# Second layer with its weights held in the array and 512 tokens moving, the result by features, and x and the result turned by 32x32 transposes and DRAM round trips

## The reference

```python
nx = _layer_norm(x, ln_gamma, ln_beta)
q = nx @ Wq;  k = prototype_bank @ Wk;  v = prototype_bank @ Wv
weights = softmax(einsum('bth,bph->btp', q, k) * H ** (-0.5))
evidence = einsum('btp,bph->bth', weights, v)
combined = concatenate([nx, evidence, anchor], axis=-1)          # 3H wide
router_probs = softmax(combined @ router_W + router_b)           # E = 3 experts
h = silu(einsum('btc,ecr->bter', combined, e_w1) + e_b1)         # R = 512 per expert
expert_out = einsum('bter,erh->bteh', h, e_w2) + e_b2
routed = sum(expert_out * router_probs[..., None], axis=-2)
g = sigmoid(silu(combined @ gate_w1 + gate_b1) @ gate_w2 + gate_b2)
return x + g * (routed @ out_w + out_b)
```

## Time and profile before

| | |
|---|---|
| median of 3 runs | 466.26 us (465.49 to 466.45) |
| span of the profiled execution | 462.2 us; the median run is 4.1 us above it |
| PE busy | 451.3 us, 98% |
| DVE busy | 263.2 us, 57% |
| ACT busy | 236.0 us, 51% |
| POOL busy | 143.4 us, 31% |
| SyncE's DMA queue | 31.76 MB in 24256 packets, 26.4% of the 16 engines' span |

### The profile page before, as it was taken

The page is one execution under the profiler, slowest core; times in us unless marked ns, Lnnn a source line. Parts: engine busy times, 40 slices in busy tenths (PEclk is TensorE's granted clock), DMA queues, the critical chain, the costliest instruction groups (busy, mean ns, idle before and its releaser), DMA issues.

```text
span 462.2 us, 7383 instructions
## 1 busy us (share of the span) xinstructions
PE 451.3 (98%) x2771; PEld 400.3 (87%) x2771; DVE 263.2 (57%) x574; ACT 236.0 (51%) x361; POOL 143.4 (31%) x200
## 2 busy tenths in 40 slices
PE   4999999999999999999999999999999999999995
PEld 4588888898988899898988999898988998988895
DVE  3567366758566554648456554648456655425336
ACT  1337455675645456634755456544754555644341
POOL 4104701009505620293005520392006520282000
PEclk9999999999999999999999999999999999999998
DMA  8577406121221322222311322222310312221001
GB/s 239 194 214 265 138 2 139 22 45 25 88 60 36 68 93 46 47 48 68 92 23 24 68 92 48 45 48 70 91 37 10 70 46 48 45 47 47 0 1 45
DMA packets 24611, 32.78 MB, mean 71 GB/s; under 512 B 1864, under 2 KB 16000, under 8 KB 24576
## 3 DMA queue, kind: packets, MB, share of 16 engines
q1 hardware_dynamic: 24256, 31.76, 26.4%
q0 software_dynamic: 240, 0.53, 0.5%
q10 hardware_dynamic: 80, 0.02, 0.0%
HBM read 13.40 MB, written 4.19 MB: 38 GB/s over the span
## 4 chain that ended last, share of the span: by engine, by line
PE 96%; DMA 1%; DVE 1%; issue 0%; SPq 0%; ACT 0%
PE bank L418 37%; PE bank L674 34%; PE bank L650 11%; PE bank L516 2%; PE bank L446 2%; PE bank L429 2%; PE bank L559 2%; PE bank L483 1%; DMA work<-in_ctx_dram 1%; PE bank L528 1%; PE bank L448 1%; PE bank L587 1%; PE bank L469 1%; PE bank L504 1%; PE bank L540 1%; PE bank L459 1%
## 5 line engine op out<-in xcount | busy, mean ns | idle before, releaser
L418 PE MATMUL bank<-nx,w1n 128*128 128x512 f32 x672 | 175.7, 397 | 0.0
L1106 DVE TENSOR_TENSOR h<-hf,h 128x512 fp32r<-128x512 f32 x112 | 83.5, 745 | 160.2 <-ACT h L828 159.3
L674 PEld LDWEIGHTS bank<-w,h 128*128 128x128 f32 x1152 | 149.8, 190 | 8.2
L674 PE MATMUL bank<-w,h 128*128 128x256 f32 x1152 | 152.0, 282 | 0.0
L825 ACT ACTIVATE hf<-bank,zb 128x512 f32<-128x512 f32 x112 | 77.2, 689 | 144.1 <-PE bank L650 143.9
L418 PEld LDWEIGHTS bank<-nx,w1n 128*128 128x128 f32 x672 | 119.3, 188 | 19.8
L828 ACT ACTIVATE h<-bank,zb 128x512 fp32r<-128x512 f32 x112 | 76.2, 681 | 0.0
L650 PE MATMUL bank<-wT,vw 128*128 128x512 f32 x224 | 69.9, 393 | 0.0
L1140 POOL TENSOR_TENSOR rstd<-ve,minus_half 128x4 f32<-128x4 f32 x8 | 9.1, 1136 | 159.1 <-DVE ve L853 159.1
L650 PEld LDWEIGHTS bank<-wT,vw 128*128 128x128 f32 x224 | 41.9, 188 | 9.0
L1150 POOL TENSOR_SCALAR work<-b2o,ph 128x256 f32<-128x256 f32 x32 | 20.8, 649 | 78.3 <-DVE ph L933 76.0
(11 more groups left out here) (127 smaller groups left out, 407.0 us busy)
## 6 DMA issues: line engine op xcount, KB each, us to landing
vw<-vw_pair SPq DMA_DIRECT2D x48, 256.0 KB, 3.7
stage<-in_L_xcond_e_w_dram SPq DMA_DIRECT2D x9, 512.0 KB, 4.5
xbuf<-in_x_dram SPq DMA_DIRECT2D x8, 512.0 KB, 4.4
out_dram<-xbuf SPq DMA_DIRECT2D x16, 256.0 KB, 2.1
vw<-vw_pair SPq DMA_DIRECT2D x16, 130.0 KB, 2.6
w1v<-in_L_xcond_e_w_dram SPq DMA_DIRECT2D x3, 512.0 KB, 6.3
work<-in_ctx_dram SPq DMA_DIRECT2D x1, 512.0 KB, 6.0
stage<-in_L_xcond_gate_w_dram SPq DMA_DIRECT2D x2, 256.0 KB, 9.6
```

The costliest lines, as they stand in the source:

```text
L418: mm = pe.matmul(dst, lhs(a), rhs(c), start=first and i == 0, stop=last and i == n - 1)
L674: mm = pe.matmul(o, h[:, s % HRING, a, t * PART:(t + 1) * PART], rhs, start=c == 0 and i == 0 and t % 2 == 0, stop=c == COUNT[g] - 1 and i ...
L1106: dve.tensor_tensor(h[:, s % HRING, LO, :], hf[:, s % 2, :], h[:, s % HRING, HI, :].bitcast(F32), ALU.subtract).then_inc(s_hlo, 1)
```

## The change

Seven edits belong together.

1. Second layer. The weights (128 hidden units by 128 output features) are held and the 512 tokens of `h` move: 2 feature halves by 3 passes, 6 matmuls of 512 columns for a slot. The result lies by features: two PSUM banks for each group, a feature on each partition and 512 tokens along it.
2. Combining. The bias is one number on the partition now (`b2o`), and the router's probability is a row of 512 tokens that has to stand on all partitions (`p_bc`). The probabilities are transposed on VectorE (`phT`), written to DRAM (`store_p`) and read back to all partitions (`load_p`). `bias_sum` is gone; the gate's bias goes into the tanh, which reads PSUM; GpSimd gets the products with the gate (`gate_factor`, `gate_third`, `gated_pair`) and the addition of x.
3. x. TensorE's transposes of x (L429) remain for batch 0 only. For batches 1 to 7 the normalised x is written to DRAM (512 KB), read back in four DMAs so that each quarter of the features lies in one group of 32 partitions (`turn_x`, pieces of 64 floats), and transposed in 32x32 blocks by one VectorE instruction (`x_turn`), which is followed by gamma and beta.
4. Result. The sum is transposed in 32x32 blocks (`y_turn`), x is read a second time in the same four-part form (`load_xq`), added, and stored in four DMAs of pieces of 64 floats.
5. Start. Since features lie in another order on the partitions, the first-layer weights for nx, the router's weights, `out_w`, gamma, beta and two biases are loaded in permuted order: four DMAs in the place of one for `stage` ("n") and `out_w`. The product of the second biases (`b2_product`) is 4 small matmuls in the place of 6 with 256 columns.
6. Order. `stats` stands behind slot 7 and `normalise` behind slot 9; `x_turn` behind slot 13 (batch 1: slot 5 of batch 0), `y_turn` behind slot 3; the tanh one slot earlier.
7. End. The last batch's first two experts are summed, gated, transposed and added to x behind slot 110 (`all_but_last`, four instructions of 128x1024), and the last expert in two halves.

```diff
-        XBUFS = 3
-        xbuf = sb("xbuf", [PART, XBUFS, NT, H])
+        xn = sb("xn", [PART, NT, H])
+        xq = sb("xq", [PART, NJ, H // QUADS])
+        quad = sb("quad", [PART, NJ, H // QUADS])
...
@@ SyncE's queue
+            def turn_x(b):
+                sp.wait_ge(s_xhat, b + 1)
+                if b > 1:
+                    sp.wait_ge(s_xhr, 16 * QUADS * (b - 1))
+                sp.dma_start(xhat_dram.rearrange("(t p) h -> p t h", p=PART), xn[:, :, :]).then_inc(s_xhw, 16)
...
+                sp.wait_ge(s_xhw, 16 * b)
+                for q in range(QUADS):
+                    sp.dma_start(quad_of(quad, q), quad_view(xhat_dram, q)).then_inc(s_xhr, 16)
+            def load_xq(b):
+                if b >= 1:
+                    sp.wait_ge(s_out, 16 * QUADS * b)
+                for q in range(QUADS):
+                    sp.dma_start(quad_of(xq, q), quad_view(x[b], q)).then_inc(s_xq, 16)
...
-            load_x(2)
+            store_p(0)
             load_staged("w2", 1)
             load_staged("n", 3)
+            load_p(0)
+            turn_x(1)
+            load_x(2)
             load_vw(0, 2)
             load_staged("c", 3)
             load_staged("w2", 2)
             load_vw(0, 3)
+            load_xq(0)
...
             for b in range(B):
-                for g in range(NG):
-                    if b + 1 < B:
-                        load_vw(b + 1, g)
-                    if g == 0 and b >= 1:
-                        store(b - 1)
-                        if b + 2 < B:
-                            sp.wait_ge(s_out, 32 * b)
-                            load_x(b + 2)
+                more = b + 1 < B
+                if more:
+                    load_vw(b + 1, 0)
+                if b >= 1:
+                    load_p(b)
+                if more:
+                    load_vw(b + 1, 1)
+                if b >= 1:
+                    store(b - 1)
+                    load_xq(b)
+                if more:
+                    load_vw(b + 1, 2)
+                if b + 2 < B:
+                    turn_x(b + 2)
+                    if b + 3 < B:
+                        load_x(b + 3)
+                if more:
+                    store_p(b + 1)
+                    load_vw(b + 1, 3)
@@ TensorE, second layer
-                    for t in (2 * half, 2 * half + 1):
-                        o = bank[AB[u % 3]][:, (t % 2) * H:(t % 2 + 1) * H]
-                        for i, (a, w) in enumerate(SPLIT_PASSES):
-                            rhs = gw2[:, w, c, :] if g == 0 else w2[:, w, j - GB, :]
-                            mm = pe.matmul(o, h[:, s % HRING, a, t * PART:(t + 1) * PART], rhs,
+                    o = bank[AB[u % 3]][:, :]
+                    half = slice(m * PART, (m + 1) * PART)
+                    for i, (w, a) in enumerate(SPLIT_PASSES):
+                        lhs = gw2[:, w, c, half] if g == 0 else w2[:, w, j - GB, half]
+                        mm = pe.matmul(o, lhs, h[:, s % HRING, a, :], start=c == 0 and i == 0,
+                                       stop=c == COUNT[g] - 1 and i == 2)
@@ VectorE
+            def x_turn(b):
+                dve.wait_ge(s_xhr, 16 * QUADS * b)
+                dve.wait_ge(s_nhi, KC * b)
+                dve.wait_ge(s_nlo, KC * b)
+                dve.transpose(nxf_blocks, quad_blocks).then_inc(s_turn, 1)
+                dve.wait_ge(s_turn, b)
+                for k in range(KC):
+                    affine(b, k, nxf[:, k, :])
...
+            def all_but_last():
                 b = B - 1
...
+                link(dve.tensor_tensor(acc, acc, tmp, ALU.add))
+                dve.wait_ge(s_tgp, KC * B)
+                link(dve.tensor_tensor(acc, acc, tg, ALU.mult))
+                dve.wait_ge(s_o, KC * b)
+                link(dve.transpose(quad_blocks, acc_blocks))
+                dve.wait_ge(s_xq, 16 * QUADS * B)
+                link(dve.tensor_tensor(xq[:, :, :], xq[:, :, :], quad[:, :, :], ALU.add))
```

More of the change, by code:

```diff
@@ new lines, in load_xq, with store_p @@
+            def load_xq(b):
[3 more added lines that the diff above has]
+                    sp.dma_start(quad_of(xq, q), quad_view(x[b], q)).then_inc(s_xq, 16)
+            def store_p(b):
+                sp.wait_ge(s_ph, b + 1)
+                if b >= 1:
+                    sp.wait_ge(s_pbc, 32 * b)
+                rows_et = prob_dram.rearrange("e (t n) -> (e t) n", n=PART)
+                for q in range(QUADS):
+                    part = slice(q * QROWS, (q + 1) * QROWS)
+                    sp.dma_start(rows_et[:, part], phT[q * QROWS:q * QROWS + E * NT, :]).then_inc(s_pw, 16)
@@ L810, in _ @@
             act.wait_ge(s_gw2, 16)
-            act.copy(gw2[:, HI, :, :], gw2_raw).then_inc(s_gwhi, 1)
+            for k in range(GB):
+                act.copy(gw2[:, HI, k, :].rearrange("p (m q a) -> p m q a", m=KC, a=QROWS), quad_cols(gw2_raw[:, k, :]))\
+                   .then_inc(s_gwhi, 1)
             exp_router(0)
@@ L1039, in _, with expert @@
             router_prob(0)
[L1042 to L1045 removed]
+            def expert(b, g, m, dst, weight):
+                u = 2 * (NG * b + g) + m
                 dve.wait_ge(s_acc, u + 1)
[L1047 to L1064 removed]
```

430 lines of the change are left out of this document (242 added, 188 removed).

## The result

The changed kernel takes 472.83 us in the median (471.17 to 473.65, 4 runs) beside 465.88 for the kernel before on the same chip: ratio 1.0156, 95% interval 1.0125 to 1.0187. It is 1.6% slower where 1.5% faster was forecast, and outside the range. The profiled execution took 473.65 us and spans 471.8. It is the slowest of the four. Every execution of the changed kernel and of the experiments takes about 1.8 us more than its span, so the profile of before, with a span of 462.2, is one of about 464.0 us, a fast one. The two profiles are therefore 9.6 us apart where the medians are 7.0 apart, and the losses read from their rows are together about 2.6 us too large.

What follows compares the result with a forecast made beforehand. TensorE, 98% busy, was taken to bound the kernel. Terms -6.4 - 6.2 + 1.0 + 4.8 = -6.8 took the span from 462.2 to 455.4 us; the median forecast was 459.5, 1.5% less, eight-in-ten range 456 to 467.

Steps and rivals of the forecast that it cites:

- Second layer, -6.4: Second layer: six matmuls of 512 columns replace twelve of 256, saving 0.057 us in each of 112 slots, 6.4 us.
- transposes, -6.2: TensorE's transposes of x: seven of eight go, at 0.89 us each, saving 6.2 us.
- Middle of the run: Round trip of x through DRAM and VectorE's changed work in mid-run: x arrives in time, nothing counted.
- it has room: VectorE in a batch: its work changes little and at 57% busy it can take the new instructions.
- slot 0's low part: VectorE's step waiting behind `x_turn`; TensorE needs it only in slot 2, so some 3 us of lateness is hidden.
- Start, +1.0 with bounds -0.3 to +5: Batch 0: 0.3 us gained at the biases' product against about 1.3 us of wait for `vw`; +1.0 us together.
- The other permuted loads are four issues for one: Start: these loads come 1.5 to 2 us later, users come over 4 us after landing; nothing counted.
- The copy of `vw`: Batch 0, second expert: queued behind batch 1's round trip, lands at 59.5 us, TensorE waits about 1.3 us.
- The queue of batch 0: Rival: small-piece reads and the next x hold the `vw` copy by 5 us for 1.3; 463.2 us, chance 0.11.
- End, +4.8: Last slots: VectorE's late work, with TensorE's wait, adds 2.6 us and the four-part store 2.2; +4.8 us.

Runs made afterwards that it cites:

- 9: Kernel of 8 with batch 2's turn of x moved from the end of batch 0 to slot 1 of batch 1, its splits to slot 3; 459.43 us, ratio 0.9876.
- 11: Kernel of 3 with each staged load of first-layer rows as one DMA instead of four, so the first layer multiplies wrong rows; one run, 468.94 us.
- 3: Changed kernel with the load of x for batch 1 issued ahead of a staged load; 471.25 us, ratio 1.0139 to the kernel before.
- experiment 5: Changed kernel with three loads issued earlier: x of batch 1, expert 0's second-layer weights, second expert's `vw` copy; 462.71 us, ratio 0.9956 to the kernel before.
- experiment 4: Kernel before the change with the biases' product moved behind the first layer's x product, so TensorE has a gap; 468.41 us, ratio 1.0084.
- 8: Kernel of 6 with the last batch's 32x32 transposes and addition of x moved behind the last slot's split; 461.47 us, ratio 0.9928 to the kernel before.
- 10: The combined version: kernel of 9 with GpSimd held back as in 7 and the end's steps spread over three slots; 457.54 us, ratio 0.9843 to the kernel before.
- 6: Kernel of experiment 5 with four added fp32 matmuls of 256 columns filling TensorE's gap, result unused; 463.14 us, ratio 0.9958 to the kernel before.
- 7: Kernel of 6 with GpSimd's gate products of batch 0 held until batch 1's router logits are read; 462.70 us, ratio 0.9949 to the kernel before.
- 12: Kernel of 10 without the four added matmuls, so only moves of existing work differ from the changed kernel; 459.84 us, ratio 0.9873 to the kernel before.
- 2: Changed kernel with the second expert's `vw` copies issued ahead of the round trip's reads; 466.70 us, ratio 1.0052 to the kernel before.
- 1: Changed kernel with four added fp32 matmuls of 256 columns behind the biases' product, closing TensorE's gap; 471.95 us, ratio 1.0158 to the kernel before.

## Why the prediction was wrong

- **Second layer, -6.4, and transposes, -6.2: right in the main.** A group takes 1.37 us, and seven rows of transposes are gone. A plain slot gains 0.046 us by the starts, 5.2 in 112 for 6.4, and 0.8 us more was given back at two slots.
- **Middle of the run: the transfer right, "it has room" of VectorE wrong.** The read landed in 2.8 us. But room over a batch says nothing of the place: slots 1 to 3 of batch 1 cost 3.3 us, 2.2 of it by this row (9). I had measured the slack ahead of `x_turn` (13 us) and named "slot 0's low part" behind it, and I left out ScalarE's `nx_hi`, which waits for it with the silus behind.
- **Start, +1.0 with bounds -0.3 to +5: this step failed.** At slot 8 it is 10.7 behind, plus the 1.3 that eight slots and one row of transposes should have gained: 12.0 us. About 0.5 of it lies ahead of the first product of x. Three things failed in it.
  1. "The other permuted loads are four issues for one [...] I count nothing." That priced the issues, not the queue's load. The weights of expert 0 were late because of them (11) and of x of batch 1 (3), which the same change issues at 24.5 us instead of 8.5, into the busiest stretch. In the diff that was a buffer fewer (`XBUFS` gone).
  2. The copy of `vw`: issue expected at 55, measured 60.1. The mechanism was right and its size wrong. The write was issued at 50.1 and not 44.6, since slots 2 and 3 were 5 us late already (43.8 in experiment 5, where they are on time), and took 7.4 us and not 4.4 beside 1.3 MB of other loads. PE waited 3.9 us for the 1.3 of the sum (whose own terms, 59.5 less 58.4, give 1.1), and slots 6 and 7 lost 6.7 with the clock. The rival "The queue of batch 0" put 5 us of wait on this copy and comes nearest. But it named the small reads and the next x, and these took 2.5 us (57.55 to 60.10) where 2.8 were reckoned; it was the late write. The 5 us of slots 0 to 2 stand in no rival.
  3. No term for the clock. Every wait was priced at its length. In this profile the granted clock is 0.50 and 0.57 in two windows of 8 us; experiment 4 puts the surcharge at about 2 us for a wait of 2.
- **End, +4.8: right**, 5.1 measured, with its two terms off by +0.7 and -0.5.

Summed with the measured terms: 12.0 - 6.3 - 6.2 + 3.3 + 1.8 + 5.1 = 9.7, and the span is 9.6 us longer. Here 6.3 is 111 slots at 0.057 us, and 1.8 what the slots from 8 on gained less than the sum has, outside slots 1 to 3 of batch 1. By experiments, as differences of ratios: the start 9.3 us (5), the end 1.4 and 1.5 together with GpSimd's hold (8, 10), batch 1 2.4 (9). The combined version is 1.6% faster than before. That this is close to the 1.5% of the forecast is in part luck: its end costs 2.9 us where 4.8 were forecast, while it loses 1 us in batch 1 and, in its profile, 1.6 us to the half clock at the start, which the forecast did not have.

The Trainium skill ("SBUF — State Buffer", section "Who interferes with whom") states that a VectorE instruction with two SBUF inputs and a GpSimd instruction that reads SBUF hold one port in turn. The trace agrees: beside GpSimd's products 0.69 us became 1.79, and one of GpSimd's of 1.3 became 2.16. I had compared only the sums of the two engines' work.

Still open: why experiments 6 to 8 and 10 show a short half clock between 34.6 and 39.8 us with no wait of PE ahead of it, why the gap of 1.15 us is followed by half clock in some profiles only, what the last 1 us of batch 1 is, and which of the loads ahead of the staged weights weighs most.

## What to carry to other kernels

When a change puts transfers into an in-order queue, follow each later transfer of that queue to its user again, in the stretch where the engines' DMA share is already near 1, and price each late one at its wait plus the clock behind it (here between nothing and about the wait again). A fix at one late transfer can be given back at the next, so repair all of them before judging a change by its time. Where an engine's step is moved, look at what queues on the engine that waits for it, not only at the step's own slack.

## What the runs showed of the hardware

- **The clock.** Half clock lasted between 3.4 and 10.2 us each time. Behind the gap ahead of the transposes of the softmax weights (near 30 us) it came after 1.93 us (4) and, with 1.15 us, in two profiles (the changed kernel, 12) and not in four (2, 3, 5, 11). With a wait at slot 6 it came for 1.9 us (3), 3.9 (the changed kernel) and 5.0 (11), and not for 1.7 (1). At 34.6 to 37.2 us it came in seven profiles: four had no wait there (6, 7, 8, 10), and it lasted 3.4 us as with 1.3 us of wait (3); with waits of 2.0 and 2.2 us (1, 2) it lasted 6.8. So waits go with half clock, and longer ones with more of it, but the length of the wait alone does not decide whether it comes. That it varies so may be why the times spread more than those of before; this is argued, since each kernel has one profile.
- **Small pieces.** SyncE's queue has 53024 packets and 17.9 MB more, 337 B each on average. Its packets took 26.4% of 16 x 462.2 us and take 43.8% of 16 x 471.8, 1354 us more: 26 ns for each, against 80 ns for the 1309 B of before. The cost goes by bytes far more than by count.
- **32x32 transposes** of fp32 on VectorE take 1.24 us for 1024 columns and 0.71 for 512, the price of an addition.
